# First attention's weights normalised ahead of the value product, and the product transposed

## The reference, cut to what matters

```
q, k = unit(xn @ Wq), unit(xn_kv @ Wk)          # 64 channels per head
sim  = 8 * q @ [null_k; k].T + alibi            # 64 x 66, causal
w    = exp(sim - max(sim)); w = w / sum(w)      # over the 66 keys
o    = w @ [null_v; v]                          # 64 tokens x 64 channels
x1   = x + concat(o over 16 heads) @ Wout       # 1024 -> 256 channels
```

## Time and profile before

| | |
|---|---|
| Median of 3 runs (lowest, highest) | 2394.07 us (2382.17, 2394.28) |
| The profiled execution | 2393.55 us |
| Its span, first to last instruction | 2391.8 us |
| Busy: PE, DVE, ACT, POOL | 2053.0, 1605.2, 1346.9, 792.1 us |
| Mean granted clock of TensorE | 0.955 of full speed |
| The step from 1059.67 to 1093.40 us: PE and DVE busy | 30.52 and 24.22 us |

### The profile page before, as it was taken

The page is one execution under the profiler, slowest core; times in us unless marked ns, Lnnn a source line. Parts: engine busy times, 40 slices in busy tenths (PEclk is TensorE's granted clock), DMA queues, the critical chain, the costliest instruction groups (busy, mean ns, idle before and its releaser), DMA issues.

```text
span 2391.8 us, 68791 instructions
## 1 busy us (share of the span) xinstructions
PE 2053.0 (86%) x26950; PEld 1564.9 (65%) x26950; DVE 1605.2 (67%) x4704; ACT 1346.9 (56%) x2834; POOL 792.1 (33%) x711
## 2 busy tenths in 40 slices
PE   5789998888888888888988888988888988889873
PEld 3667766666666666666666666666666666666652
DVE  4556676776676666666767667667666667667755
ACT  3455656655655655655665565665565665556542
POOL 1332333333333333333333333333333333333312
PEclk8999999999999999999999999999999999999975
DMA  4011111111111111111111111111111111111110
GB/s 134 10 24 30 31 30 35 32 33 29 33 33 28 33 33 28 33 33 29 32 35 28 31 35 28 31 35 28 31 35 26 33 35 28 30 35 34 24 39 22
DMA packets 330034, 79.39 MB, mean 33 GB/s; under 512 B 276014, under 2 KB 328718, under 8 KB 329742
## 3 DMA queue, kind: packets, MB, share of 16 engines
q1 hardware_dynamic: 329742, 74.77, 14.6%
HBM read 41.17 MB, written 33.55 MB: 31 GB/s over the span
## 4 chain that ended last, share of the span: by engine, by line
PE 51%; ACT 22%; DVE 18%; issue 7%; SPq 1%; POOL 0%; DMA 0%; DVEq 0%; ACTq 0%; POOLq 0%
PE pa L454 17%; ACT bd L797 4%; PE ps L500 4%; PE pa L461 3%; PE pa L433 3%; PE pc L559 3%; PE ps L598 3%; DVE qn L1080 3%; DVE nrm L1071 3%; PE ps L461 2%; PE pb L657 2%; PE pb L433 2%; DVE xnTs L1150 2%; ACT xnT L805 2%; PE ps L486 2%
## 5 line engine op out<-in xcount | busy, mean ns | idle before, releaser
L1227 POOL TENSOR_TENSOR rn<-nrg,mhalf 128x16 f32<-128x16 f32 x128 | 372.7, 2912 | 688.7 <-DVE nrg L1074 688.7
L454 PE MATMUL pa<-wq,xnTs 128*128 128x512 f32 x768 | 237.2, 456 | 78.6 <-DVE xnTs L1150 78.6
L746 ACT ACTIVATE sq<-pa 128x512 f32<-128x512 f32 x256 | 157.3, 614 | 220.6 <-PE pa L454 220.6
L757 ACT ACTIVATE qp<-pa,qks 128x512 f32<-128x512 f32 x128 | 86.9, 682 | 272.1 <-PE pa L461 272.1
L1150 DVE TENSOR_TENSOR xnTs<-xnT,xnTs 128x256 fp32r<-128x256 f32 x64 | 45.5, 711 | 288.0 <-ACT xnTs L809 288.0
L454 PEld LDWEIGHTS pa<-wq,xnTs 128*128 128x128 f32 x768 | 156.1, 217 | 126.2 <-DVE xnTs L1150 93.5
L486 PE MATMUL ps<-wout,qp 128*64 128x256 f32 x2048 | 235.1, 382 | 3.3 <-ACT pnT L838 3.3
L454 PE MATMUL pa<-wk,yTp 128*128 128x512 f32 x768 | 196.6, 405 | 0.1
L486 PEld LDWEIGHTS ps<-wout,qp 128*64 128x64 f32 x2048 | 141.2, 137 | 79.0 <-issue 9.8
L1232 POOL TENSOR_TENSOR yn<-yn,gb 128x256 f32<-128x256 f32 x64 | 47.4, 740 | 417.4 <-DVE yn L1047 417.4
L1071 DVE TENSOR_REDUCE nrm<-sq 128x16 f32<-128x1024 f32 x128 | 155.1, 1212 | 18.7 <-ACT qn L747 15.1
(11 more groups left out here) (228 smaller groups left out, 5183.0 us busy)
## 6 DMA issues: line engine op xcount, KB each, us to landing
xin<-in_x SPq DMA_DIRECT2D x64, 128.0 KB, 2.3
x1d<-x SPq DMA_DIRECT2D x64, 128.0 KB, 1.7
kxdr<-kxn SPq DMA_DIRECT2D x64, 128.0 KB, 1.7
vm<-kxdr SPq DMA_DIRECT2D x128, 64.0 KB, 2.7
odr<-o SPq DMA_DIRECT2D x256, 32.0 KB, 2.0
on<-odr SPq DMA_DIRECT2D x64, 128.0 KB, 2.1
xb<-x1d SPq DMA_DIRECT2D x64, 128.0 KB, 2.1
out<-res SPq DMA_DIRECT2D x64, 128.0 KB, 1.9
```

The source lines that it names most:

```text
L454: last = mm(bank, part(lhs(a_, k)), part(rhs(b_, k)), start=(n == 0), stop=(n == 3 * CK - 1))
L746: fn(sq[:, cols_], pa[:, 2 - 2 * h, :], ACT.Square)
L757: fn(qT[:, 4 * h:4 * h + 4, :].rearrange("p r t -> p (r t)"), pa[:, h, :], ACT.Identity, bias=0.0, scale=qks[:, 0:1]).then_inc(S("qT_done" ...
L1227: g.tensor_tensor(rn[:, n, :], nrg[:, n, :], mhalf[:, :], ALU.pow)\
```

## The change

- The first attention's weights are normalised before they are used. DVE sums all 66 weights of each head, takes the reciprocal, multiplies `pr` by it in place and copies the null weights into `pn`; PE's transposes of `pr` wait for that (`pr_norm`, `pn_done`) instead of for the exponentials (`probs`). The later denominators, the scaling into `on` and the product for `pn` go.
- `pn` is transposed right behind `pr`, and `pnT` is evacuated right behind `pT`.
- In the value product `vcat` is the stationary operand (64 columns, the column of ones is gone) and `pT` moves, so that the product is channels by tokens. The 8 transposes of `on` go. ACT evacuates the product straight into `oT`, with tokens and pairs exchanged.
- Every head now lies at the rows that `Wout` has for it, in both sequences, so that the output projection is 8 products of 128 rows and needs one copy of `wout`. Two of the start's loads go.
- The transposes of `xn` move between the two value projections, and ACT's `xnT` and `xnTs` ahead of its copies of the values. The value products are no longer split around a transpose of `kxT`.

The diff, cut to its core:

```diff
             ld("wq_in", raw_w["wq"], in_chunks("L0_attn_Wq"))
-            wo_pairs = A["L0_attn_Wout"].rearrange("(r e d) n -> e d r n", e=2, d=DH)
-            ld("late_in", wout[:, 0, :, :], A["L0_attn_Wout"].rearrange("(r p) n -> p r n", p=P))
-            ld("late_in", wout[0:DH, 1, :, :], wo_pairs[1])
-            ld("late_in", wout[DH:P, 1, :, :], wo_pairs[0])
+            ld("late_in", wout[:, :, :], A["L0_attn_Wout"].rearrange("(r p) n -> p r n", p=P))
             ld("late_in", alibi[:, :, :, :], A["alibi"])
...
                     for r in range(r0, r0 + 4):
-                        for s in range(BT):
-                            mm(ps[s * L:(s + 1) * L, 2, 0:C], oT[:, r, s * L:(s + 1) * L], wout[:, s, r, :],
-                               start=(r == 0), stop=False)
+                        mm(ps[:, 2, 0:C], oT[:, r, :], wout[:, r, :], start=(r == 0), stop=False)
...
-                def head_out(r, t, s, n):
+                def head_out(r, t, s):
                     rows = ps[s * L:(s + 1) * L, :, :]
-                    return rows[:, t, r * n:(r + 1) * n] if r < R7 else rows[:, 2, t * n:(t + 1) * n]
+                    return rows[:, t, r * J:(r + 1) * J] if r < R7 else rows[:, 2, t * J:(t + 1) * J]
...
                     rows = slice((t ^ s) * DH, (t ^ s) * DH + DH)
-                    return mm(head_out(r, t, s, J), qT[rows, r, s * L:(s + 1) * L],
+                    return mm(head_out(r, t, s), qT[rows, r, s * L:(s + 1) * L],
                               kcat[rows, r, s, t * NN:t * NN + J],
...
-                    rows = slice(t * L, (t + 1) * L)
-                    return mm(head_out(r, t, s, V1), pT[rows, r, s * L:(s + 1) * L],
-                              vcat[rows, 1 - p, r, t ^ s, :],
-                              start=True, stop=True, skip_group_check=True)
+                    rows, head = slice(t * L, (t + 1) * L), slice((t ^ s) * DH, (t ^ s) * DH + DH)
+                    return mm(ps[head, s, r * L:(r + 1) * L], vcat[rows, 1 - p, r, t ^ s, :],
+                              pT[rows, r, s * L:(s + 1) * L], start=True, stop=True, skip_group_check=True)
...
                         .then_inc(S("v_mm"), 1)
+                    wait(pe, "xn_done", i)
+                    to_T(two(pa[:, 1, :], 0), xn).then_inc(S("xnT_mm"), 1)
                     wait_part(pe, "k_raw", i, 2, 2)
...
                 if at_:
-                    wait(pe, "probs", ta)
+                    wait(pe, "pr_norm", ta)
+                    wait(pe, "pn_done", ta)
                 if c:
...
                                                    keys_of(r), ident[:, :])
-                    last.then_inc(S("pT_mm"), 1)
+                    nc.tensor.transpose(ps[0:H * NN, 2, C:C + P], pn[:, :, :].rearrange("p h n -> p (h n)"),
+                                        ident[:, :]).then_inc(S("pT_mm"), 1)
                 if c:
...
                     last.then_inc(S("mix_scores"), 1)
-                if a:
-                    wait(pe, "xn_done", i)
-                    to_T(two(pa[:, 1, :], 0), xn).then_inc(S("xnT_mm"), 1)
                 if b:
...
                 if b:
-                    nc.tensor.transpose(two(pb, 0)[:, 0, :], kxT[:, 0, :], ident[:, :])
-                if at_:
-                    for n, (r, t, s) in enumerate(HEADS):
-                        last = pv_tile(r, t, s)
-                        if n == 1:
-                            last.then_inc(S("pv_shared"), 1)
-                    wait(pe, "pv_shared", ta)
-                if b:
-                    nc.tensor.transpose(two(pb, 0)[:, 1, :], kxT[:, 1, :], ident[:, :]).then_inc(S("kxn_mm"), 1)
-                if at_:
-                    for s in range(BT):
-                        last = pv_tile(R7, 1, s)
+                    from_T(two(pb, 0), kxT).then_inc(S("kxn_mm"), 1)
+                if at_:
+                    for r in range(HP):
+                        for t, s in ((0, 0), (1, 1), (1, 0), (0, 1)):
+                            last = pv_tile(r, t, s)
                     last.then_inc(S("pv_mm"), 1)
...
                     four(pa[:, 1, :], kn, 0).then_inc(S("kT_mm"), 1)
-                if at_:
-                    wait(pe, "on_done", ta)
-                    onf = on[:, :, :, :].rearrange("p r t d -> p (r t d)")
-                    four(ps[:, 0, :], onf, 0)
-                    four(ps[:, 1, :], onf, 4)
-                    wait(pe, "pn_done", ta)
-                    nc.tensor.transpose(ps[0:H * NN, 2, C:C + P], pn[:, :, :].rearrange("p h n -> p (h n)"),
-                                        ident[:, :]).then_inc(S("oT_mm"), 1)
                 if d:
...
                 if a:
+                    wait(act, "xnT_mm", i)
+                    for k in range(CK):
+                        last = fn(xnT[:, k, :], pa[:, 1, k * P:(k + 1) * P], ACT.Identity,
+                                  bias=cols[:, NBI, k:k + 1], scale=cols[:, NG, k:k + 1])
+                    last.then_inc(S("xnT_done"), 1)
+                    wait(act, "xnT_done", i)
+                    fn(part(xnTs[:, 0, :, :]), xnT[:, :, :], ACT.Copy).then_inc(S("xnT_high"), 1)
+                if a:
                     for h in range(2):
                         wait_part(act, "v_mm", i, h + 1, 2)
-                        fn(vcat[:, p, :, h, 0:DH], pa[:, 2 - 2 * h, :].rearrange("p (r d) -> p r d", d=DH),
+                        fn(vcat[:, p, :, h, :], pa[:, 2 - 2 * h, :].rearrange("p (r d) -> p r d", d=DH),
                            ACT.Copy).then_inc(S("vbd_done"), 1)
...
                     wait(act, "pT_mm", ta)
-                    fn(pT[:, :, :].rearrange("p (b r) t -> p b (r t)", b=2), ps[:, 0:2, :], ACT.Copy)\
-                        .then_inc(S("pT_done"), 1)
+                    fn(pT[:, :, :].rearrange("p (b r) t -> p b (r t)", b=2), ps[:, 0:2, :], ACT.Copy)
+                    fn(pnT[:, :], ps[0:H * NN, 2, C:C + P], ACT.Copy).then_inc(S("pT_done"), 1)
                 if c:
...
                     fn(sT[:, :, :].rearrange("p q n -> p (q n)"), pc[:, :], ACT.Copy).then_inc(S("sT_done"), 1)
-                if a:
-                    wait(act, "xnT_mm", i)
-                    for k in range(CK):
-                        last = fn(xnT[:, k, :], pa[:, 1, k * P:(k + 1) * P], ACT.Identity,
-                                  bias=cols[:, NBI, k:k + 1], scale=cols[:, NG, k:k + 1])
-                    last.then_inc(S("xnT_done"), 1)
-                    wait(act, "xnT_done", i)
-                    fn(part(xnTs[:, 0, :, :]), xnT[:, :, :], ACT.Copy).then_inc(S("xnT_high"), 1)
                 if b:
...
                 if at_:
-                    wait(act, "oT_mm", ta)
-                    fn(oT[:, :, :].rearrange("p (b r) t -> p b (r t)", b=2), ps[:, 0:2, :], ACT.Copy)
-                    fn(pnT[:, :], ps[0:H * NN, 2, C:C + P], ACT.Copy).then_inc(S("oT_done"), 1)
+                    wait(act, "pv_mm", ta)
+                    fn(oT[:, :, :].rearrange("p r (s l) -> p s r l", s=BT),
+                       ps[:, 0:2, :].rearrange("p s (r l) -> p s r l", l=L), ACT.Copy).then_inc(S("oT_done"), 1)
                 if a:
...
                     wait(dve, "probs", ta)
-                    v.tensor_reduce(den[:, :].rearrange("p (r t) -> p r t", t=2), nulls, AX, ALU.add).then_inc(S("null_sum"), 1)
+                    heads = pr[:, :, :, :].rearrange("p r t j -> p (r t) j")
+                    v.tensor_reduce(den[:, :], heads, AX, ALU.add).then_inc(S("den_done"), 1)
+                    wait(dve, "den_done", ta)
+                    v.reciprocal(rden[:, :], den[:, :]).then_inc(S("rden_done"), 1)
+                    wait(dve, "rden_done", ta)
+                    v.tensor_tensor(heads, heads, bc(rden[:, :], 2, J), ALU.mult).then_inc(S("pr_norm"), 1)
+                    wait(dve, "pr_norm", ta)
+                    v.tensor_copy(pn[:, :, :].rearrange("p (r t) n -> p r t n", t=2), nulls)\
+                        .then_inc(S("pn_done"), 1)
                 if a:
...
                     choose()
-                if at_:
-                    wait(dve, "pv_mm", ta)
-                    wait(dve, "null_sum", ta)
-                    head = ps[:, 0:2, 0:R7 * V1].rearrange("p t (r v) -> p t r v", v=V1)
-                    tail = ps[:, 2, 0:2 * V1].rearrange("p (t v) -> p t v", v=V1)
-                    by_slot = lambda z: z[:, :].rearrange("p (r t) -> p t r", t=2)
-                    v.tensor_tensor(by_slot(den2)[:, :, 0:R7], head[:, :, :, DH], by_slot(den)[:, :, 0:R7], ALU.add)
-                    v.tensor_tensor(by_slot(den2)[:, :, R7], tail[:, :, DH], by_slot(den)[:, :, R7], ALU.add)\
-                        .then_inc(S("den_done"), 1)
-                    wait(dve, "den_done", ta)
-                    v.reciprocal(rden[:, :], den2[:, :]).then_inc(S("rden_done"), 1)
-                    wait(dve, "rden_done", ta)
-                    ont = on[:, :, :, :].rearrange("p r t d -> p t r d")
```

(19 more changed lines are left out.)

3 lines of the change are left out of this document (1 added, 2 removed).

## The result

The kernel after takes **2613.81 us** (median of 4 runs, 2611.34 to 2618.9) beside 2391.03 us (4 runs, 2382.17 to 2394.28): a ratio of 1.093, 95% interval 1.0895 to 1.0965. The forecast was 2550 us with a range of 2480 to 2625. The sign held and the block on DVE did what was forecast. The size was 64 us short: the time lies outside the forecast's own range of 2515 to 2590 and inside the band of rival (a), 2610 to 2650.

What follows compares the result with a forecast made beforehand. One chain through the first attention's weights' transposes, query projection and DVE's stretch to `qn` was taken as the bound, with PE waiting for DVE at step end. 2393.6 + 148 - 1 + 12 = 2552, said as 2550 us; range 2480 to 2625.

Steps and rivals of the forecast that it cites:

- rival (a): Both new PE idle stretches bring the lower clock every time; 1.0 to 1.5 us more per step, 2610 to 2650; chance 0.10.
- 148 - 1 + 12: Forecast's sum in us: 148 for longer steps at unchanged clock, 1 less for start loads, 12 for the lower clock.
- (e): Value products take turns because both row halves write to both PSUM banks; 0.9 us x 63 = 57, 2607; chance 0.04.
- The block: DVE's sum, reciprocal, product and copy ahead of the weights' transposes start these 3.86 us later, bounds 3.6 to 4.2.
- From the transposes to `sT`: Old 4.45 us plus 0.27 for the null weights' transpose and evacuation; query projection 2.9 us late.
- The 0.52 us given back behind `gs`: Nine transposes gone between `gs` and `omT`; `omT` starts at `gs` + 0.05, step 2.4 us longer.
- The output projection: 16 passes instead of 32 at 115 ns each save PE 1.84 us, all going into the wait for `qn`.
- +12: Lower clock in nearly every step: 0.7 us for each of 60 steps, 42, less 30 that go; bounds -30 to +150.
- (b): Faster: TensorE sets the end of the step, so removed transposes and projection count; 0.1 us per step, 2370; chance 0.05.
- (d): Nothing: delay and removed work cancel, without the clock's part; 2394 to 2400 us; chance 0.02.
- (c): Part of the wait absorbed: sum and product at half price, or block ahead of key norms; 2475 us; chance 0.08.
- the drain: The end of the run, with one first attention beside a first half missing; its cost was counted as zero.

Runs made afterwards that it cites:

- run 3: Kernel before plus 72 throw-away transposes (144 PE instructions) in the start, ahead of the loop: 2331.68 us, ratio 0.9733.
- run 8: Kernel before with only the early `xn` transposes (and ACT's `xnT` and `xnTs` ahead of `vcat`), plus 144 PE instructions in the start: 2277.72 us, ratio 0.9513.
- run 6: run 1 without DVE's sum, reciprocal and product; transposes wait for the exponentials, only the copy into `pn` is left: 2260.96 us, ratio 0.9474.
- run 1: Kernel after plus 32 throw-away transposes (64 PE instructions) in the start, ahead of the loop: 2505.21 us, ratio to before 1.0489.
- run 11: run 1 with half of the output projection (products of pairs 2, 3, 6 and 7) left out: 2558.65 us, ratio 1.0692.

## Why the prediction was right in sign and short in size

**The whole, in medians.** The runs were made in several sessions whose medians of before lie between 2388 and 2393 us, so each difference is good to some 5 us. Before 2391 to run 3, 2332: -59, supply. To run 8, 2278: -54, the early `xn`. To run 6, 2261: -17 (9 by the ratios to before), the transposed product, the wide projection and the missing transposes of `on`. To run 1, 2505: +244, the block with the clock that it brings. To after, 2614: +109, supply. With supply out on both sides the change costs 2505 - 2332 = **173 us (181 by the ratios); the forecast's terms gave 148 - 1 + 12 = 159**. The other 50 of the 64 us missed are the difference in supply, 109 - 59. The prediction had no term for it, and its upper bound had room for part of rival (a) and for (e), of which (e) did not come and (a) only in part. That 2614 still lies under 2625 is luck.

**The block, right.** Forecast were transposes 3.86 us later in the step; they start 17.03 us from its start (1133.91 - 1116.88) against 13.00 (1072.67 - 1059.67), 4.03 later, 0.18 of it because the sum begins that much later in this step. That sets an odd step against an even one. Like with like and with supply out, medians of runs 3 and 1, they start 4.0 us later in odd steps (13.1 to 17.0) and 4.6 in even ones (12.9 to 17.5). Every duration came out within 0.02 us.

**From the transposes to `sT`, right at full clock.** 4.45 + 0.27 = 4.72 us forecast; run 6 has 4.70 (1253.17 to 1257.87), and the step of run 1 at full clock has 4.54 (1390.85 to 1395.39). In after it is 5.51, since the transposes and the mixing run at the lower level. The projection behind it is 3.7 us later than in the earlier trace rows, not 2.9, and 2.7 later in that step of run 1 (1395.78 - 1373.82 against 1112.65 - 1093.40): this is where the clock's price enters. The whole step of run 1 at full clock takes 36.36 us where 36.1 were forecast.

**The 0.52 us given back behind `gs`, right**: 1.22 before, 0.71 now. **The banks**: 64 value products take 1.16 us with mixed banks, 60 took 1.15 before; rival (e) is refuted. Taken one by one, the passes of after start four at a time within 0.02 us and the next four 0.058 us on, about what one pass of 64 columns takes by itself (a quarter of the output projection's 0.216 us below), so the four quarters of the array run at once. By the order of the code a row tile of each half then writes to each of the two banks, without a price, so the rule of the Trainium skill that the prediction set against the change (TensorEngine Tiling, Restrictions and Gotchas) costs nothing that this trace shows.

**The output projection, wrong.** The prediction took "the same moving width at 115 ns each" and saved 1.84 us. 16 passes of 128 rows take 3.62 us and 32 passes of 64 took 3.67: 226 ns against 115. The two sequences' products had run side by side: taken one by one they start in pairs 0.006 us apart, a pair every 0.216 us, and after has a single pass every 0.216 us. A row of 32 merged passes does not show that. The error cost the forecast nothing, since it put the saving into the wait, which stayed at 0.72 us instead of 2.4. A real saving there would not have been free: run 11 saved 1.81 us and lost 53 us.

**The clock, fair but for supply.** The "+12" knew nothing of supply. In the middle window after has 0.93 and before 0.98. Stretches at the lower level add up to 439 us in after, 314 in run 1, 215 before and 155 in run 3 (over the whole execution). Of after's, 24 stretches with 160 us begin within 5 us behind a jump back, of run 1's none. In run 1 most steps with such a stretch take 37.0 to 37.4 us and one without takes 36.4, so 0.6 to 1.0 each over 51 steps: 0.7 for each of 60 was a fair price.

**Supply, missed.** No step of the prediction asks where the loop's code lies, although the trace of before had 272 instruction packets and an idle PE at the head of every even step, shown as an ACT wait of 1.66 us and as "issue". Rival (a) names the measured time, 2610 to 2650, but its mechanism makes only part of it: run 1 keeps both of its waits and is 109 us faster. (b) and (d) fall with run 11: the end of the step is DVE's. (c) falls with the block's rows.

**Open.** Which of the loop's blocks is dropped and fetched again, and why the stall of 1.9 us at the jump is followed by 2.84 us in one place and by 0.2 to 0.5 in another, was not taken apart. What makes up the remaining 14 us between 159 and 173 is not shown; the drain, counted as zero, took 8 us more (237.2 us from the start of step 61 in run 1, 229.0 in run 3).

## What to carry to other kernels

A normalisation on the way into a product on the critical chain cost its whole length in every step here, and the clock on top: price it from the place of its first instruction in its engine's queue, and move that before anything else (98 us for a moved block). Compare kernels with a hardware loop only beside their count of instruction packets: 144 idle instructions ahead of the loop were worth 61 us in one kernel and 64 were worth 109 in the other. Do not count work removed ahead of a wait as free: the longer wait can bring the lower clock to what follows.

## What the runs showed of the hardware that was not expected

- **Code placement.** PE's instructions come in packets of 16 KB. A loop of 1680 recorded PE instructions was fetched again in every pass (about 9 packets) in two of the places tried, and in none of the passes in others; the stall at the jump back is 1.9 us, in one of the two bad places with another 2.7 to 2.8 us behind the first four instructions. Places that differ by 256 PE instructions behave alike (2505 and 2509 us).
- **Side by side.** 32 passes of 128x64 stationary by 256 moving take 3.67 us, since two of them run at once; 16 of 128x128 by 256 take 3.62.
- **Less work, more time.** Halving the output projection raised the time from 2505 to 2559 us, with the granted clock down from 0.938 to 0.904. Less work and a longer wait are one edit here, so the run does not tell which of them lowers the clock.
